# Delta rule: sums of squares taken in two rounds of four matmuls on the four column groups

## The reference, cut to what matters

```python
q = silu(causal_conv(x @ Wq, conv_q)).reshape(bsz, seq_len, 8, 128)
k = silu(causal_conv(x @ Wk, conv_k)).reshape(bsz, seq_len, 8, 128)
n = sqrt(sum(x * x, axis=-1))            # over the 128 elements of a head
q, k = q / max(n_q, 1e-6), k / max(n_k, 1e-6)
...
state = a * (state - b * retained * k) + b * v * k     # step by step over time
out = state @ q
```

## Time and profile before

| what | us |
|---|---|
| median of 3 runs | 4056.18 |
| lowest and highest of them | 4041.48 and 4058.17 |
| span of the profiled execution, first to last instruction | 4054.5 |
| TensorE (PE) busy in the span | 3480.2 |
| VectorE (DVE) busy | 2420.3 |
| ScalarE (ACT) busy | 1593.8 |
| GpSimd (POOL) busy | 537.6 |

### The profile page before, as it was taken

The page is one execution under the profiler, slowest core; times in us unless marked ns, Lnnn a source line. Parts: engine busy times, 40 slices in busy tenths (PEclk is TensorE's granted clock), DMA queues, the critical chain, the costliest instruction groups (busy, mean ns, idle before and its releaser), DMA issues. The chain is left out here.

```text
span 4054.5 us, 124079 instructions
## 1 busy us (share of the span) xinstructions
PE 3480.2 (86%) x55256; PEld 2205.5 (54%) x55256; DVE 2420.3 (60%) x6248; ACT 1593.8 (39%) x2941; POOL 537.6 (13%) x564
## 2 busy tenths in 40 slices
PE   3877777679999998899977796999999999999985
PEld 1326665225555555555556342666666666666672
DVE  3757776337777667767775112566666666666545
ACT  1653333345444444444320243444434344443323
POOL 1212222000000000000000000222222222222210
PEclk9896667789888888989765797999999999999967
DMA  2000000121111111111000001000000000000000
GB/s 88 0 0 1 1 1 1 43 72 51 47 39 36 41 36 44 41 44 34 13 3 3 16 0 44 2 3 3 3 2 2 3 3 3 3 3 3 2 3 23
DMA packets 37030, 77.12 MB, mean 19 GB/s; under 512 B 7696, under 2 KB 11153, under 8 KB 35473
## 3 DMA queue, kind: packets, MB, share of 16 engines
q1 hardware_dynamic: 36496, 69.17, 5.3%
HBM read 64.83 MB, written 4.33 MB: 17 GB/s over the span
## 5 line engine op out<-in xcount | busy, mean ns | idle before, releaser
L1366 PE MATMUL ps<-g_hs,g_fc 128*128 128x512 f32 x448 | 276.0, 701 | 40.9 <-ACT g_hidden L1488 22.0
L1488 ACT ACTIVATE g_hidden<-ps 128x512 f32<-128x512 f32 x224 | 133.3, 595 | 383.9 <-PE ps L1366 383.3
L2133 PE MATMUL ps<-d_hp,d_w_k 128*128 128x512 f32 x512 | 282.5, 638 | 0.0
L1257 PEld LDWEIGHTS ps<-g_Q,g_K 32*32 32x32 f32 x12288 | 193.8, 114 | 144.9 <-issue 57.3
L2211 POOL TENSOR_TENSOR d_sq<-d_QK 128x512 f32<-128x512 f32 x128 | 133.0, 1039 | 934.0 <-ACT d_QK L2262 772.7
L1257 PE MATMUL ps<-g_Q,g_K 32*32 32x32 f32 (+1 forms) x12288 | 225.1, 218 | 34.4 <-issue 10.1
L1380 PE MATMUL ps<-g_hidden,g_proj 128*128 128x512 f32 x448 | 243.0, 636 | 0.0
L2231 ACT ACTIVATE d_F<-ps 128x128 f32<-128x128 f32 x256 | 70.8, 276 | 352.9 <-PE ps L2042 349.6
L1225 POOL COPY g_xb<-X 128x512 f32<-128x512 f32 x8 | 7.3, 907 | 1232.4 <-DVE X L1686 1121.5
L2406 DVE SCALAR_TENSOR_TENSOR d_conv<-ps,w_conv_q,d_conv 128x511 f32<-128x511 f32 (+2 forms) x192 | 142.3, 741 | 34.2 <-ACT d_conv L2256 30.3
L1366 PEld LDWEIGHTS ps<-g_hs,g_fc 128*128 128x128 f32 x448 | 79.5, 210 | 149.1 <-ACT g_hidden L1488 80.5
(11 more groups left out here) (479 smaller groups left out, 7885.7 us busy)
## 6 DMA issues: line engine op xcount, KB each, us to landing
g_hs<-gate_rows SPq DMA_DIRECT2D x56, 256.0 KB, 3.6
g_fc<-in_c_fc_dram SPq DMA_DIRECT2D x56, 256.0 KB, 4.1
g_proj<-in_c_proj_dram SPq DMA_DIRECT2D x56, 256.0 KB, 2.8
X<-in_x_dram SPq DMA_DIRECT2D x1, 2048.0 KB, 11.0
w_c_fc<-in_c_fc_dram SPq DMA_DIRECT2D x1, 2048.0 KB, 8.0
w_c_proj<-in_c_proj_dram SPq DMA_DIRECT2D x1, 2048.0 KB, 12.4
ex_root<-gate_rows SPq DMA_DIRECT2D x1, 2048.0 KB, 15.0
h_rows<-k SPq DMA_DIRECT2D x1, 2048.0 KB, 6.3
```

The lines of the kernel that those rows point to most:

```text
L1257: ins = e.matmul(later(scored, n_), keys_, queries(n_, planes, r_, 4 * i + j), start=(turn_ == 0 and part == 0 and n_ != 1), stop=(part == 1),
L1366: e.matmul(P[2], fc[:, n % 2, ts(f, C)], hs[:, n % 2], start=True, stop=True).then_inc(pe.steps, pe.did(now(f"u{i}")))
L1488: e.activation(r[:, slot], P[2], ACT.Relu).then_inc(act.steps, act.did(now(f"r{i}")))
L2133: ins = e.matmul(b, w_k[:, j, ts(H, C)], hp_of(u)[:, j:j + T], start=(j == 0), stop=(j == TAPS - 1))
```

## The change

The squares matmuls of the eight arrays are gathered in two rounds of four. A round runs when its fourth array is squared: the arrays 0 to 3 in turn 5 of the chunk 1, the arrays 4 to 7 in turn 5 of the chunk 3. In a round, array j goes to column group j with a [128, 32] stationary matrix, and lands in the partitions 32j to 32j+31 of the same bank. VectorE then copies all 128 partitions, and the four turning matmuls take all 128 rows against a [128, 8] matrix `heads` that picks the eight rows. GpSimd waits for a whole round before it uses the four buffers again. One more small weight (`heads`, 4 KB) is loaded ahead of the stage.

```diff
-        sq_rows = k.sb("d_square_rows", [8, T], stack=s)
+        sq_rows = k.sb("d_square_rows", [C, T], stack=s)
...
-                    put(u, NI * (x // 2) - 42 + 2 * (x % 2), "squares", x)
+                    if x % 4 == 3:
+                        put(u, NI * (x // 2) - 42 + 2 * (x % 2), "squares", x // 4)
...
                         elif what == "squares":
-                            e.wait_ge(pool.steps, pool.at(f"{tag}sq{x}"))
+                            e.wait_ge(pool.steps, pool.at(f"{tag}sq{4 * x + 3}"))
                             if x == 0 and u:
                                 e.wait_ge(dve.steps, dve.at(f"u{u - 1}ssq"))
-                            row = 4 * (x % 2) + x // 2
-                            e.matmul(few[0:8, :], k.w["picks"][:, row, :], squares(x), start=(x == 0), stop=(x == 7)).then_inc(pe.steps, pe.did(f"{tag}ss{x}"))
+                            for j in range(4):
+                                ins = e.matmul(few[ts(j, 32), :], k.w["picks"][:, x, :], squares(j), start=(x == 0), stop=(x == 1), tile_position=(0, 32 * j))
+                            ins.then_inc(pe.steps, pe.did(f"{tag}ss{x}"))
...
-                                ins = e.matmul(few[:, ts(i, 8)], sq_rows[:, ts(i, C)], k.w["ident"][0:8, 0:8], start=True, stop=True)
+                                ins = e.matmul(few[:, ts(i, 8)], sq_rows[:, ts(i, C)], k.w["heads"][:], start=True, stop=True)
...
                             if x >= 4:
-                                e.wait_ge(pe.steps, pe.at(f"{tag}ss{x - 4}"))
+                                e.wait_ge(pe.steps, pe.at(f"{tag}ss0"))
                             elif u:
-                                e.wait_ge(pe.steps, pe.at(f"u{u - 1}ss{x + 4}"))
+                                e.wait_ge(pe.steps, pe.at(f"u{u - 1}ss1"))
...
-                            e.wait_ge(pe.steps, pe.at(tag + "ss7"))
-                            e.tensor_copy(sq_rows[:], few[0:8, :]).then_inc(dve.steps, dve.did(tag + "rows"))
+                            e.wait_ge(pe.steps, pe.at(tag + "ss1"))
+                            e.tensor_copy(sq_rows[:], few).then_inc(dve.steps, dve.did(tag + "rows"))
...
-    o["picks"] = rows(np.eye(8, dtype=np.float32))
+    o["picks"] = rows(np.eye(2, 32, dtype=np.float32))
+    o["heads"] = np.zeros((C, 8), np.float32)
+    for x in range(8):
+        o["heads"][32 * (x % 4) + x // 4, 4 * (x % 2) + x // 2] = 1.0
```

More of the change, by code:

```diff
@@ L123 @@
     "gla": ["W_in2", "b_in2", "W_qka", "b_qka", "W_v2", "b_v2", "W_y2", "b_y2", "W_out2", "b_out2", "h0", "gla_mask"],
-    "delta": ["conv_q", "Wv3", "Wg3", "Wab3", "Wo3", "A_log", "dt_bias", "conv_v", "o_norm_w", "joins", "eye32", "upto3", "ones3", "picks"],
+    "delta": ["conv_q", "Wv3", "Wg3", "Wab3", "Wo3", "A_log", "dt_bias", "conv_v", "o_norm_w", "joins", "eye32", "upto3", "ones3", "picks", "heads"],
     "mix": ["W_r3", "W_k3", "W_v3", "mu"],
```

## The result

The change makes the kernel slower. The median is 4082.47 us over 16 runs against 4057.08 us for the kernel before over 16 runs; the ratio is 1.0058, with a 95% interval of 1.0042 to 1.0074.

What follows compares the result with a forecast made beforehand. TensorE was 95.3% busy, but the ScalarE-VectorE chain behind L2078 was taken to limit gains: 1.47 us a unit over 15 units, 22 us, span 4054.5 to 4032.5, plus 1.7 gives 4034 us (-0.54%); range 4012 to 4060.

Steps and rivals of the forecast that it cites:

- One round of four: Four squares matmuls on four column groups run abreast: 0.87 us a round, as long as one matmul; serial bound 3.5 us.
- B: Second of a unit's four chunks, holding round 0 in turn 5: L2365 at 3180.41 in place of 3180.77, gain 0.36 us.
- D: Fourth of a unit's four chunks, holding round 1 in turn 5: L2365 at 3221.01 in place of 3221.75, gain 0.74 us.
- (3): Rival: matmul passes keep program order, so a round takes 2.17 us; +17 us, 4073 us; chance 0.05.
- (4): Rival: column groups don't run side by side for 512-column streams, a round takes 3.5 us; +56 us, 4112; chance 0.03.
- The gains of the four chunks: Turn 5 gains 0.37 + 0.36 + 0 + 0.74 = 1.47 us a unit; over 15 units 22 us.
- A: First of a unit's four chunks, no round: L2406, L2368, L2078 and L2035 in turn 5 come earlier, gain 0.37 us.
- C: Third of a unit's four chunks, no round: turn 5 hangs on the ScalarE chain through L2256, gain 0.
- (1): Rival: TensorE is the bound after all; 3.9 us a unit, 59 us, so 3997; chance 0.04, a part of it 0.14.
- (2): Rival: the chain takes it all, other VectorE work and uncovered L2078 eat the gains; 0 to 12 us, 4044 to 4056; chance 0.24.
- if that is over 173, rival (2) holds: Profile sign: two equal chunks two units apart, 174.69 us before, come to about 171.8; over 173 means (2).
- What costs nothing: Turning matmuls on 128 rows, the wider copy, one 4 KB load and the buffer waits: 0 each, turning at most 8 x 8 ns a unit.

Runs made afterwards that it cites:

- three groups: Against the changed kernel: squares in three groups on column groups 0 to 2, arrays 0-2 in chunk B, 3-4 in C's wait, 5-7 in D; 4023.45 us, ratio 0.9933.
- fill_a: Changed kernel plus one useless 512-column float32 matmul a unit in turn 5 of chunk A, where TensorE also waits; 4072.38 us, ratio 1.0046.
- fill_c: Changed kernel plus one useless 512-column float32 matmul a unit in chunk C's 1.69 us wait; 4024.45 us, ratio 0.9924.
- before_no_c: Kernel before, with its two squares matmuls of chunk C left out, so part of the computation is missing; 4082.73 us, ratio 1.0080.
- serial_rounds: Changed kernel without column groups: each round is four matmuls in a row on column group 0, with the weights and copy of the kernel before; 4121.62 us, ratio 1.0171.

## Why the prediction was wrong, step by step

**One round of four: right.** The eight records of a round take 1.07 us in all, latency included, and the next matmul starts 0.91 us after the first. The rows of B, then of D, at full clock in the changed kernel, with the start of VectorE's L2367 (L2365 before):

```profile
2735.52 0.68 ACT L2258 ACTIVATE d_conv<-ps,w_conv_q 128x512 f32<-128x512 f32 x1
...
2737.02 1.07 PE L2142 MATMUL ps<-d_sq,w_picks 128*32 128x512 f32 x8
...
2737.93 0.41 PE L2079 MATMUL ps<-d_W,d_A 128*32 128x32 f32 x8
...
2738.38 0.29 DVE L2367 TENSOR_TENSOR d_r<-d_r,ps 32x128 f32<-32x128 f32 x1 [0.30 <-PE ps L2079]
```

```profile
2692.43 1.04 POOL L2213 TENSOR_TENSOR d_sq<-d_QK 128x512 f32<-128x512 f32 x1 [5.29 <-ACT d_QK L2264]
...
2695.05 0.29 DVE L2367 TENSOR_TENSOR d_r<-d_r,ps 32x128 f32<-32x128 f32 x1 [0.30 <-PE ps L2079]
```

From the start of the round to L2367 it is 1.36 us; I took 1.38. So rivals (3) and (4) are out. The Trainium skill's rule that matmuls start in program order (TensorE: Matmul & The Clock Gate, Part 3) doesn't hold in these traces: in the profile of three groups above four records of L2079 start before the second passes of squares that stand ahead of them in the program.

**The gains of the four chunks: right at full clock.** I measure each from a step that the squares don't move to the step that ends turn 5.

- B, ScalarE's L2256 to L2365: 3.25 us, now 2.86. Gain 0.39; forecast 0.36.
- D, GpSimd's last square to L2365: 3.38 us, now 2.62. Gain 0.76; forecast 0.74.
- A, L2256 to L2035: 2.71 us, now 2.21. Gain 0.50; forecast 0.37. VectorE's L2406 starts right behind L2256 now.
- C, L2406 to L2365: 1.88 us, now 1.89. Gain 0, as forecast.

Rows for A and C in the changed kernel (L2258 is L2256 before, L2408 is L2406, L2036 is L2035):

```profile
2714.62 0.68 ACT L2258 ACTIVATE d_conv<-ps,w_conv_q 128x512 f32<-128x512 f32 x1
...
2715.34 0.75 DVE L2408 SCALAR_TENSOR_TENSOR d_conv<-ps,w_conv_q,d_conv 128x511 f32<-128x511 f32 x1 [0.87 <-ACT d_conv L2258]
...
2716.83 1.16 PE L2036 MATMUL ps<-d_QK 128*128 128x128 f32 x8
```

```profile
2845.59 0.75 DVE L2408 SCALAR_TENSOR_TENSOR d_conv<-ps,w_conv_q,d_conv 128x511 f32<-128x511 f32 x1 [1.21 <-ACT d_conv L2258]
...
2847.48 0.29 DVE L2367 TENSOR_TENSOR d_r<-d_r,ps 32x128 f32<-32x128 f32 x1
```

Together 1.65 us a unit; I had 1.47. The kernel with the filled wait shows it as a whole, two units from one round to the same round:

```profile
2858.80 1.07 PE L2145 MATMUL ps<-d_sq,w_picks 128*32 128x512 f32 x8
...
3030.24 1.07 PE L2145 MATMUL ps<-d_sq,w_picks 128*32 128x512 f32 x8
```

That is 171.44 us, where it was 174.69: 1.63 us a unit, 24 us in 15 units, against the forecast 171.8 and 22 us. Rivals (1) and (2) are out too: the chain behind ScalarE does hold TensorE back, and takes just what I let it take.

**The step that failed: chunk C at "Gain 0", with idle time taken to cost nothing.** I let the matmuls of turn 5 of chunk C go at no price, since what follows them waits for another chain, and I gave idle time no price anywhere. The clock had no term in the sum. In A that was right as far as the runs show: fill_a fills the idle time there, and its ratio, 1.0046, can't be told from the changed kernel's 1.0058. In C the matmuls had a use: they kept TensorE working through a wait that it has anyway. Without them it waits 1.69 us in one piece in every second unit, and mostly the clock falls to half for what comes next. The same two units in the changed kernel:

```profile
2874.42 1.07 PE L2142 MATMUL ps<-d_sq,w_picks 128*32 128x512 f32 x8
...
3055.13 1.07 PE L2142 MATMUL ps<-d_sq,w_picks 128*32 128x512 f32 x8
```

180.71 us: 9.3 us more than the 171.44 at full clock, where the gain of two units is 3.3 us. My sign "if that is over 173, rival (2) holds" would have misled here, since it took the clock as given.

Over twelve units the account can be closed. A wait of 1.40 us for ScalarE stands in every second unit of all three kernels; its first and its seventh, in the kernel before, the changed one and fill_c:

```profile
2763.71 0.67 PE L2172 MATMUL ps<-d_OT,w_Wo 128*128 128x512 f32 x1 [1.40 <-ACT d_OT L2295]
...
3817.93 0.67 PE L2172 MATMUL ps<-d_OT,w_Wo 128*128 128x512 f32 x1 [1.40 <-ACT d_OT L2295]
```

```profile
2761.79 0.98 PE L2174 MATMUL ps<-d_OT,w_Wo 128*128 128x512 f32 x1 [1.40 <-ACT d_OT L2297]
...
3841.90 1.10 PE L2174 MATMUL ps<-d_OT,w_Wo 128*128 128x512 f32 x2 [1.40 <-ACT d_OT L2297]
```

```profile
2755.46 1.10 PE L2177 MATMUL ps<-d_OT,w_Wo 128*128 128x512 f32 x2 [1.40 <-ACT d_OT L2300]
...
3787.18 0.67 PE L2177 MATMUL ps<-d_OT,w_Wo 128*128 128x512 f32 x1 [1.40 <-ACT d_OT L2300]
```

That is 1054.2, 1080.1 and 1031.7 us. Six times the two units at full clock would be 1048.1 us before (6 x 174.69) and 1028.6 us with the rounds (6 x 171.44), taking the changed kernel to gain what fill_c gains. So, as an estimate, in these twelve units the change gains 19.5 us, and the clock takes 51.5 us where it took 6.1 us before: 26 us slower, against the 23 us by which the whole spans differ (4077.6 and 4054.5).

None of my rivals had the clock in it. The earlier trace rows showed full clock, and I took it as given.

**What costs nothing: right.** L2147 takes 265 ns a record against 261, 17.8 us in all against 17.7, and the copy of 128 partitions takes 654 ns where that of 8 took 638. One sign of the prediction missed without a part in the sum: TensorE's busy share was to fall to some 91%, and it is 94% in the middle of the changed kernel, part of it at half clock, and 95% in fill_c with its added matmul.

**What stays open.** The wait in chunk C is needed for the loss: filled, the clock stays up (in the trace of fill_c, and all its six executions took 4020 to 4027 us); made, in the kernel before, it falls. But the wait alone doesn't fix when: the clock falls for long behind six of seven such waits in the changed kernel, four of seven in before_no_c and one of seven in serial_rounds. Nor is it the length of one wait alone: the waits of 1.40 us for ScalarE and of 0.83 us in chunk A are there in fill_c, and its clock stays up. I didn't try which part of the neighbourhood of chunk C matters, nor whether the added matmul helps by cutting the wait short or by its work, and the runs don't settle either.

## What to carry to other kernels

A matmul in a place where TensorE waits anyway can cost nothing, as the squares of chunk C did, and may be what holds the clock; before taking one out, look at how long a piece of idle time it leaves, and ask what half the clock would cost behind it. When work is taken away and the time grows, read the granted clock in windows first, before looking for a new wait. If useful work can be moved, move it into the longest wait (the three groups are 0.7% faster than the kernel before) rather than out of it.

## What the runs showed of the hardware

- Four float32 streams of 512 columns on four column groups run abreast at the pace of one: the next matmul starts 0.91 us after the start of the round, against 0.95 us for one alone and 3.53 us for four in a row (serial_rounds).
- Matmuls on another column group start before the second pass of a matmul that stands ahead of them in the program: four records of L2079 at 2860.13, the second passes at 2860.25 (threes).
- In a stage where TensorE is 94% busy, the granted clock fell from 2.4 to 1.2 GHz behind six of seven waits of 1.69 us and came back 17 to 21 us later; TensorE's records fill the two windows behind such a wait (11.00 of 11.00 and 10.00 of 10.00 us). One 512-column matmul inside that wait, which left 0.71 us of it, kept the clock at 2.4 GHz. In another kernel, serial_rounds, the clock fell so behind only one of seven such waits.
